# Second layer norm: cast and square of the next token chunk issued ahead of the normalization of the current one

## The chip, the cores and the metric

The kernel runs on 8 cores of one Trainium2 chip. Each core computes one of the 8 batch entries by itself, with its own copy of the weights, and no core waits for another. The metric is the device time in microseconds (us) of the slowest core.

## The reference

The reference is one transformer layer on x of shape (8, 2048, 1024): an RWKV attention block and a mixture of experts, each behind a layer norm without learned scale. Cut to what matters:

```
x = x + attention(layernorm(x))          # time mix, k/v/r projections, wkv scan, output projection
x = x + ffn(layernorm(x))                # the second layer norm is the stage that is changed

layernorm(x): m = mean(x); v = var(x); (x - m) / sqrt(v + 1e-5)      # over the 1024 channels
ffn(h): shared = (silu(conv3(h)) * (h @ shared_up)) @ shared_down
        routed = top-2 of 16 experts by softmax(h @ router_w); expert 15 is the identity
        every other expert e: (silu(h @ gate[e]) * (h @ up[e])) @ down[e], weighted by combine[:, e]
```

## The kernel before

Everything is held with channels on the 128 partitions (8 blocks of 128 channels, `cc`) and tokens along the free axis (T = 2048). The residual `acc` is an SBUF tensor of 128 x 8 x 2048 f32 that lives through the whole kernel. The program is a row of blocks, and at each block's end all engines meet at a barrier:

- the attention block (lines 150 to 400 or so): four chunks of 512 tokens with layer norm, projections and scan;
- `blk2`, the second layer norm (lines 445 to 503), which reads `acc` and writes `ln2x` in bf16;
- `blk3`, the router (logits by TensorE at L533, softmax and top-2 on VectorE), whose result goes to DRAM;
- `blk4`, the conv and shared expert (L665 to L684), then 15 experts: gate L700, up L714, down L726, each over all 2048 tokens in four PSUM banks, with Silu at L798, the products at L768 and L769 and the adds to `acc` at L777. Behind it one DMA (L805) writes the output.

In `blk2` the 2048 tokens go in four chunks, `g_` = 0 to 3, of 512. There is one of every buffer: `accb` (the chunk in bf16), `xsqb` (its square), `m_sb` (mean), `vr_sb` (variance, then reciprocal deviation), `sgl` (a scratch row) and two PSUM banks `pc[0]` and `pc[1]`. One chunk is a chain over three engines:

1. VectorE casts 128 x 4096 elements of `acc` to `accb` (L463) and squares them into `xsqb` (L464).
2. TensorE multiplies with a matrix of ones, 8 matmuls into `pc[0]` (L494, the sum over channels) and 8 into `pc[1]` (L498, the sum of squares). Its marks are `S2_` and `SQ2_` with the chunk's number.
3. VectorE makes mean and variance with four small instructions (L466 to L470).
4. ScalarE makes the reciprocal deviation with Ln and Exp (L484, L485).
5. VectorE normalizes: for each of the 8 channel blocks a subtraction (L473) and a multiplication (L474), 16 instructions.

The order of the work is the order in which each engine's code is written; there is no scheduler. The helper `ES.do` makes every VectorE instruction wait for the one before it. TensorE waits in chunk `g_` for the square (`cast2_`) and, from chunk 1 on, for the normalization of the chunk before (`norm`). Since VectorE casts a chunk only when the chunk before is normalized, the first of these waits includes the second.

GpSimd issues nine weight loads at the start of `blk2` (L447 to L456): conv, shared up and down, router weights and bias, and four expert slots. The router's TensorE code waits for the first five.

Of the kernel before, what the change touches and what calls it, by code (L numbers as in the profile page):

```python
# [58 lines left out]
def build_one(ms, rec, stop_after="ffn", taps=(), parts=("id", "sh", "ex")):  # L59
# [31 lines left out]
    with ExitStack() as st:  # L91
# [327 lines left out]
        with ExitStack() as s2:  # L419
# [15 lines left out]
            with ExitStack() as sb2:  # L435
                eb2 = sb2.enter_context
                accb = eb2(nc.sbuf_tensor("accb", [128, CC, 512], BF16))
                xsqb = eb2(nc.sbuf_tensor("xsqb", [128, CC, 512], BF16))
                m_sb = eb2(nc.sbuf_tensor("m_sb", [128, 512], F32))
                vr_sb = eb2(nc.sbuf_tensor("vr_sb", [128, 512], F32))  # L440
                sgl = eb2(nc.sbuf_tensor("sgl", [128, 512], F32))
                pc = [eb2(nc.psum_tensor(f"pc{i}", [128, 512], F32)) for i in range(2)]
                blk2 = eb2(nc.Block())

                @blk2.gpsimd
                def _(g):
                    g.dma_start(cwS[:], cw_d.rearrange("k (cc p) o -> p (k cc) o", p=128)).then_inc(s_dwf, 16)  # L447
                    g.dma_start(suS[:], su_d.rearrange("(cc p) o -> p cc o", p=128)).then_inc(s_dwf, 16)
                    g.dma_start(sdS[:], sd_d.rearrange("(cc p) o -> p cc o", p=128)).then_inc(s_dwf, 16)
                    g.dma_start(rwS[:], rw_d.rearrange("(cc p) o -> p cc o", p=128)).then_inc(s_dwf, 16)  # L450
                    g.dma_start(rbS[:], rb_d[:]).then_inc(s_dwf, 16)
                    for m in range(4):
                        e, j = m // 3, m % 3
                        src = (gw_d, uw_d, dw_d)[j]
                        view = src[e].rearrange("(cc p) o -> p cc o", p=128)
                        g.dma_start(slot_ap(m), view).then_inc(s_dsl[m % 4], 16)  # L456

                @blk2.vector
                def _(v):
                    VS.eng = v  # L460
                    for g_ in range(4):
                        gs = slice(g_ * 512, (g_ + 1) * 512)
                        VS.do(lambda gs=gs: v.tensor_copy(accb[:], acc[:, :, gs]), f"cast{g_}")  # L463
                        VS.do(lambda: v.tensor_tensor(xsqb[:], accb[:], accb[:], OP.mult), f"cast2_{g_}")  # L464
                        v.wait_ge(s_pe, MS(f"t:SQ2_{g_}"))
                        VS.do(lambda: v.tensor_scalar_mul(m_sb[:], pc[0][:], 1.0 / C))  # L466
                        VS.do(lambda: v.tensor_tensor(vr_sb[:], m_sb[:], m_sb[:], OP.mult))
                        VS.do(lambda: v.scalar_tensor_tensor(vr_sb[:], pc[1][:], 1.0 / C, vr_sb[:],
                                                             OP.mult, OP.subtract))
                        VS.do(lambda: v.tensor_scalar_add(vr_sb[:], vr_sb[:], EPS), f"var2_{g_}")  # L470
                        v.wait_ge(s_sc, MS(f"s:rstd2_{g_}"))
                        for cc in range(CC):
                            VS.do(lambda cc=cc, gs=gs: v.tensor_tensor(sgl[:], acc[:, cc, gs], m_sb[:], OP.subtract))  # L473
                            VS.do(lambda cc=cc, g_=g_: v.tensor_tensor(  # L474
                                ln2x[:, cc, 2 + g_ * 512: 2 + (g_ + 1) * 512], sgl[:], vr_sb[:], OP.mult))
                        VS.ms[f"v:norm{g_}"] = VS.v
                    VS.do(lambda: v.memset(ln2x[:, :, 0:2], 0.0), "ln2pad")

                @blk2.scalar
                def _(s):  # L480
                    SS.eng = s
                    for g_ in range(4):
                        s.wait_ge(s_dv, MS(f"v:var2_{g_}"))
                        SS.do(lambda: s.activation(vr_sb[:], vr_sb[:], AF.Ln))  # L484
                        SS.do(lambda: s.activation(vr_sb[:], vr_sb[:], AF.Exp, scale=-0.5), f"rstd2_{g_}")  # L485

                @blk2.tensor
                def _(t):
                    for g_ in range(4):
                        t.wait_ge(s_dv, MS(f"v:cast2_{g_}"))  # L490
                        if g_ >= 1:
                            t.wait_ge(s_dv, MS(f"v:norm{g_ - 1}"))
                        for cc in range(CC):
                            inst = t.matmul(pc[0][:], ones_b[:], accb[:, cc, :],  # L494
                                            start=(cc == 0), stop=(cc == CC - 1))
                        TS_.mark(inst, f"S2_{g_}")
                        for cc in range(CC):
                            inst = t.matmul(pc[1][:], ones_b[:], xsqb[:, cc, :],  # L498
                                            start=(cc == 0), stop=(cc == CC - 1))
                        TS_.mark(inst, f"SQ2_{g_}")  # L500
# [353 lines left out]
```

## Time and profile before

| | |
|---|---|
| time, median of 2 runs | 2940.83 us (2889.86 and 2991.81) |
| the profiled execution | 2889.95 us |
| its span, slowest core (core 3) | 2888.4 us |
| spans of the other cores | 2870.7 to 2885.7 us |
| TensorE, VectorE, ScalarE busy on core 3 | 1872.4, 1278.9, 326.9 us |
| second layer norm on core 3 | from 840.7 to 953.7 us |

The trace comes from one execution, and its times count from the core's first instruction. The second row is that execution's own time. An engine's busy time is the sum of its instructions. In a row of the timeline, the number in brackets is how long the engine had been idle before the instruction, and behind the arrow stands what released it.

### The profile page before, as it was taken

The numbers are of one execution on the slowest core, as the hardware profiler recorded it, in microseconds if no ns is written. First come the engines' busy times: TensorE is split into PE (matmuls) and PEld (weight loads), VectorE is DVE, ScalarE is ACT, GpSimd is POOL, SyncE is SP. The second block draws the span as 40 slices with busy tenths as digits, with TensorE's granted clock in tenths as the row PEclk, the third lists the DMA queues.
The fourth block names the chain that finished last, engine by engine and source line by source line (L and its number), as shares of the span: only waits on it lengthen the run. The fifth ranks groups of instructions, "written<-read, shape, count | busy, mean of one in ns | idle before, by whom it ended". The sixth has DMA issues, their size and how long they took to land.

```text
span 2888.4 us, 21639 instructions; the slowest of 8 cores (2870.7 to 2888.4 us)
## 1 busy us (share of the span) xinstructions
PE 1872.4 (65%) x7648; PEld 784.1 (27%) x7648; DVE 1278.9 (44%) x1772; ACT 326.9 (11%) x551; POOL 67.9 (2%) x88
## 2 busy tenths in 40 slices
PE   2415424226022579887887888878878878888885
PEld 1202101102010234333333333333333323333332
DVE  4474574584456441242442442433433434424433
ACT  0310220310410000001001001000000010010000
POOL 0000000000010000000000000000000000000000
PEclk8656767668566789998998989989989889989887
DMA  6603404305035000032131221321321321212203
GB/s 147 97 20 51 66 0 63 53 0 88 0 45 87 17 7 1 0 51 37 16 46 23 35 37 16 51 37 15 51 37 15 52 31 21 39 25 40 30 1 116
DMA packets 69194, 112.77 MB, mean 39 GB/s; under 512 B 2480, under 2 KB 37312, under 8 KB 68048
## 3 DMA queue, kind: packets, MB, share of 16 engines
q0 software_dynamic: 63856, 94.50, 22.0%
q1 hardware_dynamic: 5232, 16.91, 1.8%
q8 instruction: 61, 1.00, 0.1%
q14 instruction: 45, 0.37, 0.1%
HBM read 197.28 MB, written 8.52 MB: 71 GB/s over the span
## 4 chain that ended last, share of the span: by engine, by line
PE 52%; DVE 9%; issue 2%; ACT 1%; DVEq 0%; DMA 0%; ACTq 0%; POOLq 0%
PE pc L700 18%; PE pc L726 16%; PE pc L714 14%; DVE h L769 4%; DVE sg L768 4%; PE pc L665 2%; PE pc L684 1%; ACT sg L798 1%; PE pc L673 1%; DVE h L739 1%; DVE acc L742 1%; DVE h L751 0%; DVE acc L777 0%; DVEq L36 0%; DMA cb<-comb_dram 0%
## 5 line engine op out<-in xcount | busy, mean ns | idle before, releaser
L700 PE MATMUL pc<-ln2x,wsl 128*128 128x512 bf16 x1920 | 519.7, 437 | 190.9 <-ACT sg L798 189.9
L768 DVE TENSOR_TENSOR sg<-sg,pc 128x512 f32<-128x512 f32 x240 | 165.0, 687 | 822.2 <-PE pc L714 803.2
L726 PE MATMUL pc<-h,wsl 128*128 128x512 bf16 x1920 | 461.5, 404 | 100.6 <-DVE h L769 99.9
L714 PE MATMUL pc<-ln2x,wsl 128*128 128x512 bf16 x1920 | 427.6, 379 | 0.0
L777 DVE TENSOR_TENSOR acc<-acc,pc 128x512 f32<-128x512 f32 x480 | 330.2, 688 | 182.8 <-PE pc L726 144.3
L700 PEld LDWEIGHTS pc<-ln2x,wsl 128*128 128x128 bf16 x1920 | 206.7, 110 | 502.8 <-issue 341.4
L798 ACT ACTIVATE sg<-pc 128x512 f32<-128x512 f32 x240 | 143.3, 597 | 1522.4 <-PE pc L700 1016.2
L726 PEld LDWEIGHTS pc<-h,wsl 128*128 128x128 bf16 x1920 | 190.2, 103 | 371.9 <-issue 192.2
L369 PE MATMUL pb<-mx,wsla 128*128 128x512 bf16 x512 | 131.6, 425 | 240.8 <-DVE mx L225 214.5
L714 PEld LDWEIGHTS pc<-ln2x,wsl 128*128 128x128 bf16 x1920 | 187.6, 98 | 230.2
L769 DVE TENSOR_TENSOR h<-sg,cb 128x512 bf16<-128x512 f32 x240 | 166.1, 692 | 25.4 <-DVE sg L768 0.5
L369 PE MATMUL pb<-sry,wsla 128*128 128x512 bf16 x256 | 66.6, 429 | 143.2 <-DVE sry L282 94.9
L369 PEld LDWEIGHTS pb<-mx,wsla 128*128 128x128 bf16 x512 | 54.1, 107 | 318.2 <-issue 279.4
L369 PE MATMUL pb<-mxb,wsla 128*128 128x512 bf16 x256 | 63.9, 416 | 64.3 <-DMA wsla<-wv 57.8
L665 PE MATMUL pc<-ln2x,cw_sb 128*128 128x512 bf16 x384 | 86.2, 386 | 9.6 <-PEq L515 6.4
L360 PE MATMUL pb<-xb,ones_b 128*128 128x512 bf16 x32 | 14.0, 618 | 102.1 <-DVE xsq L200 102.1
L369 PEld LDWEIGHTS pb<-sry,wsla 128*128 128x128 bf16 x256 | 27.2, 107 | 182.7 <-issue 164.1
L275 DVE TENSOR_TENSOR_SCAN Q_ch<-ewb,Q_ch,e_t 128x128 f32<-128x128 f32 x128 | 62.0, 484 | 13.7 <-DVE Q_ch L275 0.5
L271 DVE TENSOR_TENSOR_SCAN P_ch<-ewb,P_ch,w 128x128 f32<-128x128 f32 x128 | 62.0, 484 | 13.7 <-DVE P_ch L271 0.5
L260 DVE CAST v_sb<-pb 128x512 bf16<-128x512 f32 x32 | 22.1, 692 | 99.3 <-PE pb L369 96.4
L494 PE MATMUL pc<-accb,ones_b 128*128 128x512 bf16 x32 | 13.9, 616 | 80.3 <-DVE xsqb L464 80.3
L281 DVE TENSOR_TENSOR w<-w,e_t 128x1024 f32<-128x1024 f32 x16 | 19.6, 1226 | 97.2 <-ACT e_t L328 97.2
(119 smaller groups left out, 922.8 us busy)
## 6 DMA issues: line engine op xcount, KB each, us to landing
wsl<-gw POOLq DMA_DIRECT2D x15, 1024.0 KB, 10.1
wsl<-uw POOLq DMA_DIRECT2D x15, 1024.0 KB, 10.4
wsl<-dw POOLq DMA_DIRECT2D x15, 1024.0 KB, 10.1
acc<-x SPq DMA_DIRECT2D x4, 2048.0 KB, 24.6
wsla<-wk POOLq DMA_DIRECT2D x4, 2048.0 KB, 17.1
wsla<-wv POOLq DMA_DIRECT2D x4, 2048.0 KB, 18.4
wsla<-wr POOLq DMA_DIRECT2D x4, 2048.0 KB, 28.2
wsla<-wo POOLq DMA_DIRECT2D x4, 2048.0 KB, 16.7
```

The source lines that it names most:

```text
L271: VS.do(lambda cc=cc: v.tensor_tensor_scan(P_ch[:, cc, 1:], ewb[:, cc, :], w1[:, cc, :], P_ch[:, cc, 0:1], OP.mult, OP.add))
L275: VS.do(lambda cc=cc: v.tensor_tensor_scan(Q_ch[:, cc, 1:], ewb[:, cc, :], e_t[:, cc, :], Q_ch[:, cc, 0:1], OP.mult, OP.add))
L369: inst = t.matmul(pb[od][:], wsl_a[m % 2][:, kc, od * 128:(od + 1) * 128], rhs_t[:, kc, :], start=(kc == 0), stop=(kc == CC - 1))
L665: inst = t.matmul(pc4[ocI][:], cwS[:, kk * 8 + kc, ocI * 128:(ocI + 1) * 128], ln2x[:, kc, t0 - 2 + kk: t0 - 2 + kk + 512], start=(kk == 0 ...
L673: inst = t.matmul(pc4[4 + ocI][:], suS[:, kc, ocI * 128:(ocI + 1) * 128], ln2x[:, kc, t0:t0 + 512], start=(kc == 0), stop=(kc == CC - 1))
L700: inst = t.matmul(pc4[tc][:], slot_ap(3 * e)[:, kc, ocI * 128:(ocI + 1) * 128], ln2x[:, kc, 2 + tc * 512: 2 + (tc + 1) * 512], start=(kc = ...
L714: inst = t.matmul(pc4[4 + tc][:], slot_ap(3 * e + 1)[:, kc, ocI * 128:(ocI + 1) * 128], ln2x[:, kc, 2 + tc * 512: 2 + (tc + 1) * 512], sta ...
L726: inst = t.matmul(pc4[(oc % 2) * 4 + tc][:], slot_ap(3 * e + 2)[:, kcI, oc * 128:(oc + 1) * 128], h[:, kcI, tc * 512:(tc + 1) * 512], star ...
L768: VS.do(lambda sl=sl, tc=tc: v.tensor_tensor(sl[:], sl[:], pc4[4 + tc][:], OP.mult))
L769: VS.do(lambda sl=sl, e=e, ocI=ocI, tc=tc: v.tensor_tensor(h[:, ocI, tc * 512:(tc + 1) * 512], sl[:], cb[e % 2][:, tc, :], OP.mult), f"h{e ...
L777: VS.do(lambda dst=dst, ac=ac, oc=oc, tc=tc: v.tensor_tensor(dst, ac, pc4[(oc % 2) * 4 + tc][:], OP.add))
L798: SS.do(lambda idx=idx, tc=tc: s.activation(sg[idx % 2][:], pc4[tc][:], AF.Silu), f"silu{e}_{ocI}_{tc}")
```

## The change

The edit is in VectorE's and TensorE's code of `blk2`. The cast and the square of chunk 0 stand ahead of the loop. Inside the loop, the cast and the square of chunk `g_ + 1` stand between the variance of chunk `g_` and the wait for its reciprocal deviation. TensorE's wait for the normalization of the chunk before is taken out. No instruction is added, and none is dropped.

```diff
                     VS.eng = v
+                    VS.do(lambda: v.tensor_copy(accb[:], acc[:, :, 0:512]), "cast0")
+                    VS.do(lambda: v.tensor_tensor(xsqb[:], accb[:], accb[:], OP.mult), "cast2_0")
                     for g_ in range(4):
                         gs = slice(g_ * 512, (g_ + 1) * 512)
-                        VS.do(lambda gs=gs: v.tensor_copy(accb[:], acc[:, :, gs]), f"cast{g_}")
-                        VS.do(lambda: v.tensor_tensor(xsqb[:], accb[:], accb[:], OP.mult), f"cast2_{g_}")
                         v.wait_ge(s_pe, MS(f"t:SQ2_{g_}"))
...
                         VS.do(lambda: v.tensor_scalar_add(vr_sb[:], vr_sb[:], EPS), f"var2_{g_}")
+                        if g_ + 1 < 4:
+                            ns = slice((g_ + 1) * 512, (g_ + 2) * 512)
+                            VS.do(lambda ns=ns: v.tensor_copy(accb[:], acc[:, :, ns]), f"cast{g_ + 1}")
+                            VS.do(lambda: v.tensor_tensor(xsqb[:], accb[:], accb[:], OP.mult), f"cast2_{g_ + 1}")
                         v.wait_ge(s_sc, MS(f"s:rstd2_{g_}"))
...
                         t.wait_ge(s_dv, MS(f"v:cast2_{g_}"))
-                        if g_ >= 1:
-                            t.wait_ge(s_dv, MS(f"v:norm{g_ - 1}"))
```

VectorE, the first chunk of `blk2`, before. The names are those of the buffers above, and in brackets stand the semaphores of an instruction's waits (`s_pe` from TensorE, `s_sc` from ScalarE, `s_dv` VectorE's own):

```order
L463 CAST accb<-acc 128x4096 [waits s_dv]
L464 TENSOR_TENSOR xsqb<-accb 128x4096 [waits s_dv]
L466 TENSOR_SCALAR m_sb<-pc 128x512 [waits s_pe,s_dv]
L467 TENSOR_TENSOR vr_sb<-m_sb 128x512 [waits s_dv]
L468 SCALAR_TENSOR_TENSOR vr_sb<-pc,vr_sb 128x512 [waits s_dv]
L470 TENSOR_SCALAR vr_sb<-vr_sb 128x512 [waits s_dv]
L473 TENSOR_TENSOR sgl<-acc,m_sb 128x512 [waits s_sc,s_dv]
L474 TENSOR_TENSOR ln2x<-sgl,vr_sb 128x512 [waits s_dv]
```

The same place in the changed kernel:

```order
L461 CAST accb<-acc 128x4096 [waits s_dv]
L462 TENSOR_TENSOR xsqb<-accb 128x4096 [waits s_dv]
L466 TENSOR_SCALAR m_sb<-pc 128x512 [waits s_pe,s_dv]
L467 TENSOR_TENSOR vr_sb<-m_sb 128x512 [waits s_dv]
L468 SCALAR_TENSOR_TENSOR vr_sb<-pc,vr_sb 128x512 [waits s_dv]
L470 TENSOR_SCALAR vr_sb<-vr_sb 128x512 [waits s_dv]
L473 CAST accb<-acc 128x4096 [waits s_dv]
L474 TENSOR_TENSOR xsqb<-accb 128x4096 [waits s_dv]
L477 TENSOR_TENSOR sgl<-acc,m_sb 128x512 [waits s_sc,s_dv]
L478 TENSOR_TENSOR ln2x<-sgl,vr_sb 128x512 [waits s_dv]
```

The cast and the square of chunk 1 (now L473 and L474) have moved in between the variance and the first instruction that waits for ScalarE (now L477).

VectorE where chunk 0 ends and chunk 1 goes on, before (the last pair of the normalization, then what follows):

```order
L473 TENSOR_TENSOR sgl<-acc,m_sb 128x512 [waits s_dv]
L474 TENSOR_TENSOR ln2x<-sgl,vr_sb 128x512 [waits s_dv]
L463 CAST accb<-acc 128x4096 [waits s_dv]
L464 TENSOR_TENSOR xsqb<-accb 128x4096 [waits s_dv]
L466 TENSOR_SCALAR m_sb<-pc 128x512 [waits s_pe,s_dv]
L467 TENSOR_TENSOR vr_sb<-m_sb 128x512 [waits s_dv]
```

The same place in the changed kernel:

```order
L477 TENSOR_TENSOR sgl<-acc,m_sb 128x512 [waits s_dv]
L478 TENSOR_TENSOR ln2x<-sgl,vr_sb 128x512 [waits s_dv]
L466 TENSOR_SCALAR m_sb<-pc 128x512 [waits s_pe,s_dv]
L467 TENSOR_TENSOR vr_sb<-m_sb 128x512 [waits s_dv]
L468 SCALAR_TENSOR_TENSOR vr_sb<-pc,vr_sb 128x512 [waits s_dv]
L470 TENSOR_SCALAR vr_sb<-vr_sb 128x512 [waits s_dv]
```

The wait for TensorE (L466) used to follow the square directly; now the 16 instructions of the normalization stand between them. TensorE's own order is the same in both kernels.

## Rows read from the trace of the kernel before

**Rows 1.** Page: span and busy times by engine.
```profile
span 2888.4 us, 21639 instructions; the slowest of 8 cores (2870.7 to 2888.4 us)
PE 1872.4 (65%) x7648; PEld 784.1 (27%) x7648; DVE 1278.9 (44%) x1772; ACT 326.9 (11%) x551; POOL 67.9 (2%) x88
```
**Rows 2.** Waits, 840.5 to 954 us: engine, line, releaser, us in total, times, longest.
```profile
DVE m_sb L466 <- PE pc L498: 23.5, 4, 6.6
DVE sgl L473 <- ACT vr_sb L485: 8.3, 4, 2.9
```
**Rows 3.** Timeline, chunk 1: start, us, engine, line, op, [idle before, releaser].
```profile
856.69 0.69 DVE L473 TENSOR_TENSOR sgl<-acc,m_sb 128x512 f32<-128x512 f32 x1 [2.95 <-ACT vr_sb L485]
...
869.43 2.29 DVE L463 CAST accb<-acc 128x4096 bf16<-128x4096 f32 x1
871.83 2.29 DVE L464 TENSOR_TENSOR xsqb<-accb 128x4096 bf16<-128x4096 bf16 x1
...
874.38 3.57 PE L494 MATMUL pc<-accb,ones_b 128*128 128x512 bf16 x8 [23.64 <-DVE xsqb L464]
...
877.74 2.75 PE L498 MATMUL pc<-xsqb,ones_b 128*128 128x512 bf16 x8
...
880.67 0.69 DVE L466 TENSOR_SCALAR m_sb<-pc 128x512 f32<-128x512 f32 x1 [6.55 <-PE pc L498]
...
885.16 0.69 DVE L473 TENSOR_TENSOR sgl<-acc,m_sb 128x512 f32<-128x512 f32 x1 [1.67 <-ACT vr_sb L485]
```
**Rows 4.** Timeline: the same two waits in chunks 0, 2 and 3, and the stage's end.
```profile
850.91 0.69 DVE L466 TENSOR_SCALAR m_sb<-pc 128x512 f32<-128x512 f32 x1 [5.50 <-PE pc L498]
...
908.56 0.69 DVE L466 TENSOR_SCALAR m_sb<-pc 128x512 f32<-128x512 f32 x1 [5.97 <-PE pc L498]
...
913.40 0.69 DVE L473 TENSOR_TENSOR sgl<-acc,m_sb 128x512 f32<-128x512 f32 x1 [2.02 <-ACT vr_sb L485]
...
936.34 0.69 DVE L466 TENSOR_SCALAR m_sb<-pc 128x512 f32<-128x512 f32 x1 [5.52 <-PE pc L498]
...
953.60 0.07 DVE L477 MEMSET ln2x<- 128x16 bf16 x1
...
954.14 8.95 PE L533 MATMUL pc<-ln2x,rw_sb 128*16 128x512 bf16 x32 [17.98 <-PEq L435]
```
**Rows 5.** Timeline: the first cast and GpSimd's weight loads.
```profile
840.73 2.29 DVE L463 CAST accb<-acc 128x4096 bf16<-128x4096 f32 x1 [0.39 <-PEq L125]
841.06 3.00 POOL L447 DMA_DIRECT2D cw_sb<-cw  x1 [138.59 <-SPq L435]
...
846.53 0.56 POOL L451 DMA_DIRECT2D rb_sb<-rb  x1
...
849.58 0.95 POOL L456 DMA_DIRECT2D wsl<-gw  x1
```
**Rows 6.** DMA view of 780 to 1300 us: the router bias, KB, us from issue to landing.
```profile
rb_sb<-rb POOLq DMA_DIRECT2D x1, 0.1 KB, 50.1
```
**Rows 7.** One line's instructions (L742, TensorE busy beside it): ns min/median/max.
```profile
L742 DVE TENSOR_TENSOR acc<-acc,h x4: 4424/4425/4425, 1003.8 to 1031.0; 128x4096 f32<-128x4096 f32 x4
```
**Rows 8.** Window ahead of the router: us, busy PE, PEld, DVE, ACT, POOL (x), PEclk, DMA share, GB/s.
```profile
945.00:953.90 8.90, 0.00 (x0) 0.00 (x0) 7.49 (x12) 0.00 (x0) 0.00 (x0) 0.50 0.00 0
```
**Rows 9.** Chain that ended last, start and us: a gate group at its usual shortest, and the longest.
```profile
1283.49 7.06 PE pc L700 x32
...
2201.31 10.02 PE pc L700 x32
```
**Rows 10.** Page, costliest groups: the gate matmuls.
```profile
L700 PE MATMUL pc<-ln2x,wsl 128*128 128x512 bf16 x1920 | 519.7, 437 | 190.9 <-ACT sg L798 189.9
```
**Rows 11.** The gate matmuls on cores 3 and 7: count, ns, first and last start.
```profile
L700 PE MATMUL pc<-ln2x,wsl x1920: 376/379/634, 1172.2 to 2815.7; 128*128 128x512 bf16 x192
L700 PE MATMUL pc<-ln2x,wsl x1920: 376/379/634, 1155.9 to 2799.4; 128*128 128x512 bf16 x192
```

## The prediction

> **What bounds the kernel now.** I read the page first. Of a span of 2888.4 us on core 3, TensorE is busy 1872.4 and VectorE 1278.9 us [rows 1], so neither is busy throughout and the kernel is a chain of stages that hand work to each other. The stage that the change touches is the second layer norm. Its first cast starts at 840.73 us [rows 5] and its last instruction, a memset, at 953.60 [rows 4]: 112.9 us, 3.9% of the span. It ends in a barrier, and TensorE begins the router 0.5 us behind it, at 954.14, after 17.98 us of idleness [rows 4]. So what the stage gives up, the router starts earlier by.
>
> Next I read the waits of this stage. VectorE waits 23.5 us in four goes for the sums from TensorE and 8.3 us in four goes for the reciprocal deviation from ScalarE [rows 2]. These 31.8 us are all that VectorE waits there, apart from the gaps of about 0.1 us between its instructions; the other 81 us are its own work. VectorE therefore bounds the stage, with two round trips per chunk added in series. The timeline of chunk 1 shows the series [rows 3]: cast and square from 869.43, TensorE's 16 matmuls from 874.38 to 880.49, VectorE idle for 6.55 us until 880.67, four small instructions, idle for 1.67 us until 885.16, then the normalization. The reader should note that TensorE sat idle for 23.64 us before its matmuls. It has room for the sums, but gets its input too late.
>
> **The change, part by part.** All instructions and their sizes stay; only VectorE's order changes. I go through the two waits.
>
> *The wait for TensorE.* In chunk 0 nothing can be put ahead of it, so its 5.50 us [rows 4] stay. In chunks 1, 2 and 3 the square is done before the normalization of the chunk before begins. That normalization takes from 856.69 to 869.43, 12.74 us for 16 instructions of 0.69 us and their gaps (on to the start of the cast behind it) [rows 3]. TensorE's work takes 6.1 us (874.38 to 877.74 + 2.75 [rows 3]). It ends about 6 us before VectorE asks for it, so even a doubling of it would be hidden. Removed are 6.55 [rows 3] + 5.97 + 5.52 [rows 4] = 18.04 us.
>
> *The wait for ScalarE.* The cast and square of the next chunk, 4.8 us from 869.43 to 871.83 + 2.29 + gap [rows 3], now run while ScalarE works. ScalarE's part took 2.95 us in chunk 0 (with the load of its table), 1.67 in chunk 1 [rows 3] and 2.02 in chunk 2 [rows 4]. All three are shorter than 4.8 us, so 6.64 us go. Chunk 3 has no next chunk, and its wait stays.
>
> *What comes in their place.* Each of the six waits becomes an ordinary gap, 0.1 us by the pair of cast and square (871.83 - 869.43 - 2.29) [rows 3]: 0.6 us back. *The wait taken out of TensorE* costs and brings nothing by itself: what it named had to be done anyway before the new square. The moved cast writes `accb` only after TensorE has read it, and VectorE has just waited for that at L466, so no wait is added.
>
> The sum: 18.04 + 6.64 - 0.6 = 24.1 us. The memset then starts near 929.5 instead of 953.60.
>
> *The unknown costs.* First, VectorE's normalization now runs beside TensorE's matmuls, which the stage has not shown before. The nearest row is a relative of the subtraction, an addition of two SBUF operands at 128x4096 with TensorE busy beside it: 4.42 us [rows 7]. A cost of 0.69 us for 512 columns [rows 3] and 4.42 for 4096 [rows 7] differ by 1.04 ns a column, and that rate leaves 0.16 us of the 0.69 as a fixed part: a small and plausible one, so the instruction beside TensorE is not visibly slowed. I take nothing. The other end is bounded by the overlap: 3 x 6.1 = 18 us of VectorE work, and if all of it went a quarter slower, 4.6 us. Below nothing is excluded, since no operand shrinks. Second, the router starts earlier, and it needs the router bias, issued at 846.53 and landing 50.1 us behind its issue, so near 897 [rows 5, 6]. That is 33 us before 929.5, so I take nothing. Third, TensorE is idle before the router for some 24 us instead of 18: the sums of chunk 3 now end ahead of the 3 us of small instructions, the ScalarE wait and the last normalization. Its granted clock was already 0.50 in the 8.9 us before the router [rows 8], which is the lower of its two levels, 1.2 GHz. It can fall no further, so again nothing. Fourth, everything behind the router keeps its order and its gaps and shifts by 24 us.
>
> Against the profiled execution, 2889.95 - 24.1 = 2865.9 us. That execution agrees with the lower of the two runs shown (2889.86 us); their median, 2940.83, is drawn up by the other (2991.81). The ratio, 0.9917, is what I expect to hold; the absolute time holds for executions like the profiled one. A median of two that again had one run 102 us longer would be 2865.9 + 51 = 2917. A difference of 2%, 58 us, is about what a measurement of this kernel can tell from no change, so this gain lies within it.
>
> **The rivals.** *The clock takes it back (slower).* The expert stage works with pauses in which TensorE's clock falls. A gate group of 32 matmuls takes 7.06 us right behind the down projection and up to 10.02 behind a wait [rows 9]. All of L700 costs 519.7 us [rows 10]; without 15 groups of 7.06 there are 413.8 us for 45 groups, 9.20 each. If starting the stage at another moment put all 45 at 10.02, this would add 45 x 0.82 = 37 us, and the kernel would end at 2889.95 - 24.1 + 37 = 2903. The point from which it decides is 24.1 / 45 = 0.54 us per group. Against it speaks that cores 3 and 7 begin the gates at 1172.2 and 1155.9 us, 16.3 us apart, and their last gate matmul starts 1643.5 us behind the first on both [rows 11]: the groups do not care when the stage begins. The Trainium skill speaks for this rival. Its page "TensorE: Matmul & The Clock Gate", in the part on the HAM clock gate, says that the activity window is free-running and does not reset when the kernel starts; by that rule the moment of the start would matter, up to the price just worked out. The two cores' rows disagree with it at this size, so I give the rival little.
>
> *Weights late (half the gain, or none).* If the bias landed behind 929.5, the router would wait. Half of the gain is gone if it lands at 941.5, 95 us after its issue instead of 50: the time would be 2878. What speaks for it is the first load's issue, which took 3.00 us from 841.06 while the cast that began at 840.73 ran for 2.29 us; the last took 0.95 [rows 5]. The moved casts come at 853.8 and later, behind the last issue (849.58 + 0.95), but inside the time in which the loads move. If each of the three moved casts held the loads up by its length, that would be 6.9 us, landing at 903.5: still 26 us early. In the Trainium skill, "SBUF — State Buffer", section "SBUF: two separate sides", a cast in a 2-port mode locks GpSimd out while it runs and starves the descriptors of its DMAs; the 3.00 us agree, and by that rule the landing moves by no more than these 6.9 us.
>
> *The gain drowns in the other stages.* Core 3 alone sets the time, and the cores' spans lie between 2870.7 and 2888.4 us [rows 1], 17.7 us apart with the same program. If the slowest core in another execution comes 12 to 24 us later, 2878 to 2890 is measured; if all come like the fastest, 2848.
>
> *The change does not do what it says.* VectorE could still stand still at L466 if TensorE began late. It does not: its only wait is for the square, and its queue holds nothing else. I leave 2 in 100 for no gain, 2890.
>
> **How the numbers follow.** The forecast, 24 us off, gets 0.74. The gain drowned or doubled by the spread gets 0.12, half to either side; weights late 0.05; the clock rival 0.05; no effect 0.02; something unseen 0.02. The likeliest's own range is 2857 to 2875 (the 4.6 us of slower VectorE work and as much spread above, all 31.8 us of waits gone below). The range of 8 in 10 reaches down to 2850 for an execution with all cores early and up to 2920, which takes in the rivals at 2878, 2890 and 2903 and the median of two unlike runs, 2917. Faster by over 2% would need 58 us where only 31.8 us of waits exist, so only a measurement against an unlike run gives it: 0.04. Slower by over 2% needs 82 us of loss after the gain, more than the clock rival has: 0.03. Within 2%: 0.93.
>
> **What would show it right or wrong.** In the profile of the changed kernel the stage from the first cast to the memset should take 88.8 us instead of 112.9. VectorE's waits for TensorE should be one of 5.5 us, and those for ScalarE one of 1.7 us. TensorE's matmuls for chunks 1 to 3 should run beside L477 and L478, which should still take 0.69 us. The router should start 0.5 us behind the memset, with no wait for a DMA. From there to the end, the distance should be unchanged at 2888.4 - 954.1 = 1934.3 us. I am wrong if a wait for the sums above 1 us is left in chunks 1 to 3, if the normalization's instructions grow, or if that distance moves by more than 5 us.

## The result, and the profile after

The changed kernel takes 0.9924 of the time of the kernel before, with a 95% interval of 0.9911 to 0.9937. That is 22 us less (18 to 26), within the 2% that count as the same. The runs of before lie between 2889.45 and 2892.79 us, those of after between 2864.84 and 2870.55 us. Some executions of any kernel are several per cent longer, with a lower clock on the cores of one die; they are left out of every time and ratio here, and of their profiles only the cores of the other die are read.

The profiled execution took 2865.14 us, with a span of 2863.6 us on core 5. First the page: busy times are those of before to within 3.1 us, as they should be when nothing is added or dropped [rows 1].

```profile
span 2863.6 us, 21636 instructions; the slowest of 8 cores (2848.7 to 2863.6 us)
PE 1875.5 (65%) x7648; PEld 784.5 (27%) x7648; DVE 1278.9 (45%) x1772; ACT 327.0 (11%) x551; POOL 67.9 (2%) x88
```

The waits of VectorE in the stage (engine, line, what it waited for, us in total, times, longest) answer to [rows 2]. L466 is the same line as before, L477 is the former L473:

```profile
DVE m_sb L466 <- PE pc L500: 5.5, 1, 5.5
DVE sgl L477 <- ACT vr_sb L489: 1.7, 1, 1.7
```

Of four waits each, one each is left: 7.2 us where there were 31.8. The timeline from chunk 0's variance to chunk 2 answers to [rows 3] and [rows 4]:

```profile
852.12 0.69 DVE L466 TENSOR_SCALAR m_sb<-pc 128x512 f32<-128x512 f32 x1 [5.54 <-PE pc L500]
...
855.05 2.29 DVE L473 CAST accb<-acc 128x4096 bf16<-128x4096 f32 x1
855.08 1.28 ACT L488 ACT_TABLE_LOAD   x1 [38.69 <-DVE vr_sb L470]
856.38 0.63 ACT L488 ACTIVATE vr_sb<-vr_sb 128x512 f32<-128x512 f32 x1
857.10 0.63 ACT L489 ACTIVATE vr_sb<-vr_sb 128x512 f32<-128x512 f32 x1
857.45 2.29 DVE L474 TENSOR_TENSOR xsqb<-accb 128x4096 bf16<-128x4096 bf16 x1
859.85 0.69 DVE L477 TENSOR_TENSOR sgl<-acc,m_sb 128x512 f32<-128x512 f32 x1
859.89 3.57 PE L496 MATMUL pc<-accb,ones_b 128*128 128x512 bf16 x8 [7.94 <-DVE xsqb L474]
860.64 0.69 DVE L478 TENSOR_TENSOR ln2x<-sgl,vr_sb 128x512 bf16<-128x512 f32 x1
...
863.25 2.10 PE L500 MATMUL pc<-xsqb,ones_b 128*128 128x512 bf16 x8
...
872.58 0.69 DVE L466 TENSOR_SCALAR m_sb<-pc 128x512 f32<-128x512 f32 x1
...
896.32 2.29 DVE L473 CAST accb<-acc 128x4096 bf16<-128x4096 f32 x1 [0.46 <-DVE vr_sb L470]
...
918.34 0.69 DVE L477 TENSOR_TENSOR sgl<-acc,m_sb 128x512 f32<-128x512 f32 x1 [1.67 <-ACT vr_sb L489]
...
931.11 0.07 DVE L481 MEMSET ln2x<- 128x16 bf16 x1
...
931.65 8.87 PE L535 MATMUL pc<-ln2x,rw_sb 128*16 128x512 bf16 x32 [25.19 <-PEq L435]
```

ScalarE's table load and its two instructions end at 857.73, under the cast and the square, which end at 859.74. TensorE's sums run from 859.89 to 865.35, beside the normalization, and L466 at 872.58 finds them ready: the row has no bracket. The normalization's instructions still take 0.69 us with TensorE beside them. One stall is new: VectorE sits idle for 0.46 us ahead of the cast at 896.32, where the gaps between its other instructions are 0.1 us.

The stage, from the first cast at 841.89 to the memset, takes 89.2 us where it took 112.9. The profiled executions differ by 24.8 us, and it can be added up: the stage -23.65 us; the slowest core enters it 1.16 us later (841.89 and 840.73); from the memset to the issue of the output 1910.1 and 1910.3, -0.2; the output's landing 22.1 us behind its issue on core 5 and 24.2 on core 3, -2.1. The issue on core 5 is this row:

```profile
L807 SPq DMA_DIRECT2D out<-acc x1: 389/389/389, 2841.2 to 2841.2; - x1
```

### The profile page after: what moved, and what is told of

It is laid out like the page before. It is cut to its first block, busy times and chain, and to the rows that moved or that the text cites. A ratio compares the mean times of both kernels' runs of the same rounds, so it can differ in the third digit from the quotient of the medians.

```text
span 2863.6 us, 21636 instructions; the slowest of 8 cores (2848.7 to 2863.6 us)
## 1 busy us (share of the span) xinstructions
PE 1875.5 (65%) x7648; PEld 784.5 (27%) x7648; DVE 1278.9 (45%) x1772; ACT 327.0 (11%) x551; POOL 67.9 (2%) x88
## 4 chain that ended last, share of the span: by engine, by line
PE 53%; DVE 10%; issue 2%; ACT 1%; DVEq 0%; DMA 0%; ACTq 0%; POOLq 0%
PE pc L702 18%; PE pc L728 16%; PE pc L716 15%; DVE h L771 4%; DVE sg L770 4%; PE pc L667 2%; PE pc L686 1%; ACT sg L800 1%; PE pc L675 1%; DVE acc L744 1%; DVE h L741 1%; DVE acc L779 0%; DVE h L753 0%; DVEq L36 0%; DMA cb<-comb_dram 0%
## 5 line engine op out<-in xcount | busy, mean ns | idle before, releaser
L260 DVE CAST v_sb<-pb 128x512 bf16<-128x512 f32 x32 | 22.1, 692 | 99.0 <-PE pb L369 96.1
L281 DVE TENSOR_TENSOR w<-w,e_t 128x1024 f32<-128x1024 f32 x16 | 19.6, 1226 | 97.6 <-ACT e_t L328 97.6
L369 PEld LDWEIGHTS pb<-mxb,wsla 128*128 128x128 bf16 x256 | 27.0, 107 | 101.0 <-issue 77.1
```

What stands on the lines that cost most here:

```text
L369: inst = t.matmul(pb[od][:], wsl_a[m % 2][:, kc, od * 128:(od + 1) * 128], rhs_t[:, kc, :], start=(kc == 0), stop=(kc == CC - 1))
```

## The experiments

Each experiment's diff is against the changed kernel, where nothing else is said. "Stage" is the time from the first cast to the memset, and "rest" the time from the memset to the issue of the output's DMA; both are read from every core's instruction rows and named for the majority of the cores.

### TensorE's wait alone

Against the kernel before, only this:

```diff
                         t.wait_ge(s_dv, MS(f"v:cast2_{g_}"))
-                        if g_ >= 1:
-                            t.wait_ge(s_dv, MS(f"v:norm{g_ - 1}"))
```

> The kernel before, with only TensorE's wait for the normalization of the chunk before taken out; VectorE's order is that of before. Theory (the gain comes from VectorE's order, the wait was implied by the square): the stage of the second layer norm stays at 112.9 us, VectorE still waits 4 times for TensorE, 23.5 us in all, and the time stays at 2890 us. Rival (the wait itself held TensorE back): the waits for TensorE shrink by some us and the stage gets shorter than 110 us.

On cores 4 to 7 the stage takes 112.7 or 112.8 us and the rest is 1910.4 us, for 112.9 and 1910.3 us on most cores before. The waits on core 5:

```profile
DVE m_sb L466 <- PE pc L496: 23.4, 4, 6.5
DVE sgl L473 <- ACT vr_sb L485: 8.3, 4, 3.0
```

Taking the wait out does nothing while VectorE keeps its order. There is no total time of this kernel that could be compared, so this is shown for the stage and the rest alone.

### The cast behind the wait for ScalarE

```diff
+                        v.wait_ge(s_sc, MS(f"s:rstd2_{g_}"))
                         if g_ + 1 < 4:
                             ns = slice((g_ + 1) * 512, (g_ + 2) * 512)
                             VS.do(lambda ns=ns: v.tensor_copy(accb[:], acc[:, :, ns]), f"cast{g_ + 1}")
                             VS.do(lambda: v.tensor_tensor(xsqb[:], accb[:], accb[:], OP.mult), f"cast2_{g_ + 1}")
-                        v.wait_ge(s_sc, MS(f"s:rstd2_{g_}"))
```

> The changed kernel, with the cast and the square of the next chunk behind the wait for the reciprocal deviation instead of ahead of it, still ahead of the normalization. Theory (two separate round trips, 18.0 and 6.6 us): the wait for TensorE stays hidden in chunks 1 to 3, the wait for ScalarE returns in chunks 0 to 2 (2.95 + 1.67 + 1.67, less 0.3 of gaps), so the stage takes 89.2 + 6.0 = 95.2 us and the whole gain over before is 17.7 us, ratio 0.994. Rival (VectorE does not keep its pace when TensorE works beside it, and the two terms only happen to add up): the stage comes out away from 95.2 by more than 1 us.

The stage takes 95.1 or 95.2 us on seven cores, 6.0 more than with the full change. The waits on core 5:

```profile
DVE accb L474 <- ACT vr_sb L489: 6.6, 3, 2.9
DVE m_sb L466 <- PE pc L500: 5.5, 1, 5.5
DVE sgl L477 <- ACT vr_sb L489: 1.7, 1, 1.7
```

So the two terms are separate: this order keeps the whole TensorE term and gives back the ScalarE term, 6.6 us less two gaps of 0.1 us and the 0.46 us stall. Two runs took 2870.97 and 2873.04 us against 2887.4 to 2888.9 of before, which is 14 to 18 us less; they are too few for an interval. The rest was 1914.3 us on five cores and 1907.6 to 1908.1 on three, where it had been 1910.1: a clear sign that the stages behind do care.

### TensorE's wait put back

```diff
                         t.wait_ge(s_dv, MS(f"v:cast2_{g_}"))
+                        if g_ >= 1:
+                            t.wait_ge(s_dv, MS(f"v:norm{g_ - 1}"))
```

> The changed kernel, with TensorE's wait for the normalization of the chunk before put back; VectorE keeps the new order. Theory: TensorE's sums of chunks 1 to 3 can't run beside the normalization, VectorE waits about 6 us for each of them, and only the ScalarE term is left: the stage takes 89.2 + 17.5 = 106.7 us, the time is 5 to 7 us below before, ratio 0.998. The rival that TensorE's wait costs nothing once the square is early: the stage stays at 89.2 us and the ratio at 0.992.

The stage takes 108.2 to 108.4 us. Timeline of VectorE and TensorE on core 3:

```profile
870.79 3.57 PE L498 MATMUL pc<-accb,ones_b 128*128 128x512 bf16 x8 [20.69 <-DVE ln2x L478]
874.16 2.53 PE L502 MATMUL pc<-xsqb,ones_b 128*128 128x512 bf16 x8
876.87 0.69 DVE L466 TENSOR_SCALAR m_sb<-pc 128x512 f32<-128x512 f32 x1 [6.22 <-PE pc L502]
...
903.81 0.69 DVE L466 TENSOR_SCALAR m_sb<-pc 128x512 f32<-128x512 f32 x1 [6.58 <-PE pc L502]
...
931.11 0.69 DVE L466 TENSOR_SCALAR m_sb<-pc 128x512 f32<-128x512 f32 x1 [6.59 <-PE pc L502]
```

TensorE now starts when the normalization ends, and VectorE waits 24.9 us in four goes. With the new order on VectorE, this wait, which cost nothing before, costs 19 us: both halves of the edit are needed. It is 1.6 us more than expected, mostly since the three waits came to 19.4 us and not to the 18.04 us of before: fewer of the sums ran at the upper clock level (6.22, 6.58 and 6.59 us for 6.55, 5.97 and 5.52 [rows 3, 4]).

The total was a miss. The ratio to before is 1.0002 (0.9987 to 1.0016), and 0.998 was expected. The stage is 4.6 us shorter than before, but the rest is 1914.9 us on five cores against 1910.3 before and gives it back (on two cores it is 1908.1 us and on one 1918.3). This is the clock rival of the prediction, at a size that I had put aside; the rows that tie it to the clock stand in the last experiment.

### The sums made twice

```diff
-                        for cc in range(CC):
-                            inst = t.matmul(pc[0][:], ones_b[:], accb[:, cc, :],
-                                            start=(cc == 0), stop=(cc == CC - 1))
-                        TS_.mark(inst, f"S2_{g_}")
-                        for cc in range(CC):
-                            inst = t.matmul(pc[1][:], ones_b[:], xsqb[:, cc, :],
-                                            start=(cc == 0), stop=(cc == CC - 1))
+                        for rp in range(2):
+                            for cc in range(CC):
+                                inst = t.matmul(pc[0][:], ones_b[:], accb[:, cc, :],
+                                                start=(cc == 0), stop=(cc == CC - 1))
+                            for cc in range(CC):
+                                inst = t.matmul(pc[1][:], ones_b[:], xsqb[:, cc, :],
+                                                start=(cc == 0), stop=(cc == CC - 1))
                         TS_.mark(inst, f"SQ2_{g_}")
```

> The changed kernel, with all 16 matmuls of sums made twice in each chunk (the second pass writes the same sums), so TensorE's work in the stage doubles. Theory (12.7 us of normalization cover the sums): in chunk 0 VectorE waits 3.5 to 6.8 us longer (16 more matmuls at 0.218 or 0.427 us), in chunks 1 to 3 TensorE needs 9.6 to 12.9 us and VectorE waits for nothing or under 1 us. The stage takes 92.7 to 97 us. Rival (the cover is already used up, the sums are only just hidden): each of chunks 1 to 3 gets 3 us or more of wait, and the stage takes over 101 us.

The stage takes 92.6 to 93.2 us. Timeline of chunks 0 and 1, on core 3:

```profile
853.99 0.69 DVE L466 TENSOR_SCALAR m_sb<-pc 128x512 f32<-128x512 f32 x1 [8.97 <-PE pc L500]
...
861.75 3.57 PE L497 MATMUL pc<-accb,ones_b 128*128 128x512 bf16 x8 [7.94 <-DVE xsqb L474]
...
868.75 1.89 PE L500 MATMUL pc<-xsqb,ones_b 128*128 128x512 bf16 x8
874.45 0.69 DVE L466 TENSOR_SCALAR m_sb<-pc 128x512 f32<-128x512 f32 x1
```

Only chunk 0 pays, 3.5 us: VectorE has no other wait for the sums in the stage. In chunk 1 the doubled sums end at 870.64, still 3.8 us ahead of VectorE. TensorE's time in chunks 1 to 3 is free now, and apart from the first wait for TensorE and the last for ScalarE the stage is bound by VectorE alone. The one run took 2866.97 us.

### The weight loads in the other order

```diff
-                    g.dma_start(cwS[:], cw_d.rearrange("k (cc p) o -> p (k cc) o", p=128)).then_inc(s_dwf, 16)
                     g.dma_start(suS[:], su_d.rearrange("(cc p) o -> p cc o", p=128)).then_inc(s_dwf, 16)
+                    g.dma_start(cwS[:], cw_d.rearrange("k (cc p) o -> p (k cc) o", p=128)).then_inc(s_dwf, 16)
```

> The changed kernel, with GpSimd's first two weight loads in the other order: shared up (1 MB) first, conv (3 MB) second. If the first load's issue took 3.00 us because the cast held GpSimd up, the shared up load, now first and under the cast, takes until the cast's end or longer, over 2.2 us instead of 0.88, and the conv load about as long as its size asks. If the 3.00 us come from the load's own size, the shared up load stays near 0.9 us and the conv load near 3.0 us in second place. Either way the stage stays at 89.2 us and the time at 2865 to 2870 us.

Timeline of the cast and of GpSimd beside it, core 0:

```profile
840.82 2.29 DVE L461 CAST accb<-acc 128x4096 bf16<-128x4096 f32 x1 [0.39 <-PEq L125]
...
841.16 2.44 POOL L447 DMA_DIRECT2D su_sb<-su  x1 [138.75 <-SPq L435]
843.58 1.42 POOL L448 DMA_DIRECT2D cw_sb<-cw  x1
```

The same two loads in the changed kernel, core 5:

```profile
842.23 3.00 POOL L447 DMA_DIRECT2D cw_sb<-cw  x1 [138.83 <-SPq L435]
845.22 0.88 POOL L448 DMA_DIRECT2D su_sb<-su  x1
```

Both expectations named a part of it. The shared up load takes 2.44 us under the cast and 0.88 behind it; the conv load takes 3.00 under the cast and 1.42 behind it. The first place adds 1.56 us to the one and 1.58 to the other, whatever the load, and that is 0.4 us less than the 1.95 us for which issue and cast overlap (841.16 to 843.11). The swap by itself leaves one rival: the first load also follows 138.8 us in which GpSimd was idle, and could be slow for that. An earlier load of the changed kernel speaks against it:

```profile
263.50 0.87 POOL L160 DMA_DIRECT2D wsla<-wv  x1 [145.41 <-PE pb L369]
```

Behind 145.41 us of idleness, and with no cast of this length beside it, it takes 0.87 us. The load at 845.22 runs beside the square of chunk 0 and still takes 0.88 us, so it is the cast that holds the issue and not VectorE's work as such. The rule of the Trainium skill, "SBUF — State Buffer", section "SBUF: two separate sides", that such a cast locks GpSimd out, agrees with these rows. In the changed kernel no moved cast meets an issue: the last load is issued at 850.74 for 0.95 us, and the first moved cast starts at 855.05. The router bias landed 44.7 us behind its issue on core 5, for 50.1 [rows 6]. The stage is 89.1 or 89.2 us on six cores and 0.6 more on two, where without the swap one core had the 0.6 us. The one run took 2864.92 us, as expected.

### A wider normalization

```diff
-                sgl = eb2(nc.sbuf_tensor("sgl", [128, 512], F32))
+                sgl = eb2(nc.sbuf_tensor("sgl", [128, CC, 256], F32))
...
-                        for cc in range(CC):
-                            VS.do(lambda cc=cc, gs=gs: v.tensor_tensor(sgl[:], acc[:, cc, gs], m_sb[:], OP.subtract))
-                            VS.do(lambda cc=cc, g_=g_: v.tensor_tensor(
-                                ln2x[:, cc, 2 + g_ * 512: 2 + (g_ + 1) * 512], sgl[:], vr_sb[:], OP.mult))
+                        for hf in range(2):
+                            h0 = g_ * 512 + hf * 256
+                            mbc = m_sb[:, hf * 256:(hf + 1) * 256].unsqueeze(1).broadcast_to([128, CC, 256])
+                            rbc = vr_sb[:, hf * 256:(hf + 1) * 256].unsqueeze(1).broadcast_to([128, CC, 256])
+                            VS.do(lambda h0=h0, mbc=mbc: v.tensor_tensor(
+                                sgl[:], acc[:, :, h0:h0 + 256], mbc, OP.subtract))
+                            VS.do(lambda h0=h0, rbc=rbc: v.tensor_tensor(
+                                ln2x[:, :, 2 + h0:2 + h0 + 256], sgl[:], rbc, OP.mult))
```

> The changed kernel, with the normalization of a chunk in 4 instructions of 128 x 2048 (8 blocks of 256 tokens, mean and deviation broadcast over the blocks) instead of 16 of 128 x 512; the scratch tensor grows to 128 x 8 x 256 f32. Theory (VectorE alone bounds the stage now, so its fixed costs count one to one): 4 instructions at 2048 x 1.04 ns + 0.16 us = 2.29 us and 0.1 of gap each are 9.6 us for 12.74, four times: 12.6 us less. The stage takes 76.6 us, the sums (6.1 us) stay hidden, the time falls to 2853 us by the profiled execution, ratio to before 0.987. Rival (the freed time turns into waits for TensorE, since less work covers the sums): waits at L466 in chunks 1 to 3 appear, and the stage stays above 80 us.

The subtractions of the stage on core 6 (count, then busy us and mean ns of one, then idle time before them); the multiplications take the same 18.3 and 2292:

```profile
L480 DVE TENSOR_TENSOR sgl<-acc,m_sb 128x2048 f32<-128x2048 f32 x8 | 18.3, 2292 | 2.4 <-ACT vr_sb L493 1.7
```

One instruction takes 2292 ns, the expected 2.29 us. The stage takes 76.2 us on most cores (13.0 less), and the waits are again one of 5.5 and one of 1.7 us. On the engine that bounds a stage, a fixed cost of 0.16 us and a gap of 0.1 us per instruction count one to one: 48 instructions fewer make 12.5 us, and the 0.46 us stall is gone too. The ratio to before is 0.9871 (0.9856 to 0.9886), as expected, but more closely than its parts: the rest was 1912.8 us on four cores, 2.7 us longer, and 1906.0 to 1909.9 us on the others.

### And the square on ScalarE

Beside the wide normalization:

```diff
-                            VS.do(lambda: v.tensor_tensor(xsqb[:], accb[:], accb[:], OP.mult), f"cast2_{g_ + 1}")
...
+                        if g_ + 1 < 4:
+                            s.wait_ge(s_dv, MS(f"v:cast{g_ + 1}"))
+                            SS.do(lambda: s.activation(fl(xsqb[:]), fl(accb[:]), AF.Square), f"sq{g_ + 1}")
...
-                        t.wait_ge(s_dv, MS(f"v:cast2_{g_}"))
+                        t.wait_ge(s_dv, MS(f"v:cast{g_}"))
...
+                        t.wait_ge(s_sc, MS(f"s:sq{g_}"))
```

Chunk 0 is changed in the same way.

> As the wide normalization, and with the square of the chunk on ScalarE (Square from bf16 to bf16) instead of VectorE; TensorE's first 8 matmuls wait only for the cast. Theory: VectorE loses 2.4 us of work in each of chunks 1 to 3; in chunk 0 the square (about 3.5 us) runs beside the first 8 matmuls and 1 to 2 us go; the wait for ScalarE in chunk 0 comes back by 0.5 us since the cast alone covers 2.4 of its 2.95 us. The stage takes about 68.5 us, the time is 2845 us, ratio 0.984. Rival (ScalarE becomes the bound: square behind the deviation, and the activation table is reloaded at 1.28 us a switch): VectorE waits for the sums in chunks 1 to 3 and the stage stays above 74 us.

The ratio to before is 0.9834 (0.9821 to 0.9848), the fastest version of this study; its five runs took 2839.14 to 2844.01 us. Chunk 0 on core 0:

```profile
843.90 1.28 ACT L489 ACT_TABLE_LOAD   x1 [27.95 <-DVE accb L461]
843.91 3.57 PE L503 MATMUL pc<-accb,ones_b 128*128 128x512 bf16 x8 [9.24 <-DVE accb L461]
...
845.19 3.62 ACT L489 ACTIVATE xsqb<-accb 128x4096 bf16<-128x4096 bf16 x1
...
848.95 3.57 PE L508 MATMUL pc<-xsqb,ones_b 128*128 128x512 bf16 x8 [1.47 <-ACT xsqb L489]
...
852.70 0.69 DVE L465 TENSOR_SCALAR m_sb<-pc 128x512 f32<-128x512 f32 x1 [8.93 <-PE pc L508]
```

The stage takes 70.1 us on seven cores and 68.4 on one, where 68.5 was expected. What I had left out is in these rows: the table load of 1.28 us now stands ahead of the square of chunk 0, and TensorE's second eight matmuls behind its pause of 1.47 us run at the lower clock throughout (3.57 us for 1.89). On core 5, the one with 68.4 us, they follow a pause of 1.53 us and take 1.89. There is only one load in the stage, and Square, Ln and Exp alternate behind it without another. That the total came out at the expected place is luck: the rest was 1904.7 to 1905.4 us on six cores, 5 us shorter than before, and 1908.8 on the two others, the slowest core among them.

### Does the rest care when it begins?

Two kernels with idle work at the end of the stage, 2 instructions as shown, and 4:

```diff
                     VS.do(lambda: v.memset(ln2x[:, :, 0:2], 0.0), "ln2pad")
+                    for _ in range(2):
+                        VS.do(lambda: v.tensor_tensor(sgl[:], m_sb[:], m_sb[:], OP.mult))
```

> The changed kernel, with 2 more VectorE instructions of 128x512 at the end of the stage (they write a scratch row that nobody reads), which start the router 1.6 us later. Theory of the prediction (the stages behind do not care when they begin): the distance from the memset to the output's issue grows by 1.6 us, from 1910.1 to 1911.7 on most cores, and router and experts keep 39.4 and 1643.5 us. Rival (TensorE's clock level depends on the moment at which its work begins): the router part changes by 1 to 4 us, as it did in the runs with the cast behind the deviation and with TensorE's wait put back (42.3 and 42.8 us for 39.4), or the gates' stretch moves by 3 us or more on most cores.

> The same with 4 more instructions, a shift of 3.2 us. Theory of the prediction: 1913.3 us from the memset to the output's issue, router 39.4 us behind its start and gates' stretch 1643.5 us. Rival: as above; whether this shift falls on a better or a worse moment than the one of 1.6 us I can't say beforehand, only that the two runs and the changed kernel will not all agree.

With the shift of 3.2 us, six cores have a rest of 1913.6 or 1913.7 us, near the expected 1913.3 (two have 1917.6). With 1.6 us the cores fall apart: 1903.7, 1907.2, 1910.0, 1913.4 twice, 1914.0, 1916.8 and 1916.9 us, where 1911.7 was expected. The runs took 2866.85 us with 1.6 us and 2871.01 us with 3.2, one of each. The router of core 3, first in the changed kernel, then with 1.6 us, then with 3.2 us:

```profile
918.12 8.86 PE L535 MATMUL pc<-ln2x,rw_sb 128*16 128x512 bf16 x32 [25.20 <-PEq L435]
930.58 5.66 PE L541 MATMUL pc<-id_sb,lg 16*128 16x16 f32 x32 [3.60 <-DVE lg L557]
946.00 5.14 PE L547 MATMUL pc<-id_sb,ctm 128*16 128x128 f32 x32 [9.77 <-DVE ctm L579]
```
```profile
926.28 9.73 PE L537 MATMUL pc<-ln2x,rw_sb 128*16 128x512 bf16 x32 [26.82 <-PEq L435]
939.62 6.97 PE L543 MATMUL pc<-id_sb,lg 16*128 16x16 f32 x32 [3.60 <-DVE lg L559]
956.70 6.43 PE L549 MATMUL pc<-id_sb,ctm 128*16 128x128 f32 x32 [10.11 <-DVE ctm L581]
```
```profile
918.08 8.96 PE L537 MATMUL pc<-ln2x,rw_sb 128*16 128x512 bf16 x32 [28.40 <-PEq L435]
930.64 5.57 PE L543 MATMUL pc<-id_sb,lg 16*128 16x16 f32 x32 [3.60 <-DVE lg L559]
946.33 5.06 PE L549 MATMUL pc<-id_sb,ctm 128*16 128x128 f32 x32 [10.12 <-DVE ctm L581]
```

The same three pieces of TensorE work take 19.7, 23.1 and 19.6 us. They follow pauses of nearly the same length (25 to 28, 3.60 and about 10 us); what differs is the moment at which they start. Over the time from the router's first matmul to the first of the convolution (window and its length in us, then busy time of TensorE, its weight loads, VectorE, ScalarE and GpSimd, then the mean granted clock, the DMA share and GB/s), in the changed kernel and with 1.6 us:

```profile
918.10:957.50 39.40, 19.66 (x96) 12.58 (x97) 11.64 (x24) 1.70 (x2) 0.00 (x0) 0.72 0.03 4
926.30:969.50 43.20, 23.12 (x96) 14.51 (x97) 11.64 (x24) 1.70 (x2) 0.00 (x0) 0.62 0.03 4
```

VectorE and ScalarE are busy for the same time in both. The mean granted clock is 0.72 and 0.62 of full speed, and 0.72 again with 3.2 us: the upper level holds for 17.1, 10.2 and 17.1 us of the three windows. The experts move too: the gates' stretch from first to last matmul is 1643.5 us in the changed kernel and between 1633.7 and 1644.3 us on the cores with the 1.6 us shift. The shortest and the longest gates' stretch of these kernels, core 7 with the shift of 1.6 us and core 7 with TensorE's wait put back:

```profile
1139.90:2773.70 1633.80, 1348.95 (x5600) 565.81 (x5601) 633.34 (x920) 140.94 (x236) 41.33 (x54) 0.90 0.20 31
1166.70:2813.20 1646.50, 1362.57 (x5599) 569.13 (x5600) 633.34 (x920) 140.90 (x236) 41.33 (x54) 0.89 0.21 31
```

Again only TensorE's busy time differs, by 13.6 us for 12.7 us of stretch.

With the shifts the cores don't fall apart at random. Ahead of the inserted instructions, VectorE's first wait in the stage is 5.5 or 5.6 us on some cores, where the clock first rises 8.0 to 8.3 us behind the first cast, and 6.05 to 6.08 us on the others, where it rises 9.1 or 9.2 us behind it. With 1.6 us the five cores of the first kind have a router of 43.2 to 43.7 us and the three others one of 40.7 to 42.0; with 3.2 us the six of the first kind have 39.7 to 40.1 us and the two others 42.5 and 42.9. The five begin the stage between 821.0 and 835.9 us, so the router's time goes with the shift and the kind of core and not with the time since the core's start. The gates' stretch doesn't follow from them: 1637.4 to 1644.3 us on those five.

The commonest values over the kernels of this study, and where a few cores stand apart, theirs:

| kernel | stage, us | router, us | gates' stretch, us | rest, us |
|---|---|---|---|---|
| before | 112.9 | 39.5 | 1643.5, on one 1646.5 | 1910.3, on one 1913.7 |
| changed | 89.2 | 39.4 | 1643.5, on one 1640.1 | 1910.1, on one 1907.2 |
| TensorE's wait alone (four cores) | 112.8 | 39.5 | 1643.5 | 1910.4 |
| cast behind the wait for ScalarE | 95.2 | 42.4 | 1644.2 or 1643.5, on three 1637.2 | 1914.3, on three 1907.6 to 1908.1 |
| TensorE's wait put back | 108.3 | 42.8 | 1644.2, on two 1637.3 | 1914.9, on two 1908.1, on one 1918.3 |
| sums made twice | 92.7 | 39.4 | 1643.5 | 1910.0 to 1910.6, on one 1906.6, on one 1913.4 |
| weight loads swapped | 89.2 | 39.4 | 1643.5 | 1910.1, on three 1907.2, 1910.7 and 1913.5 |
| wide normalization | 76.2 | 40.7 | 1644.3 | 1912.8, on four 1906.0 to 1909.9 |
| square on ScalarE | 70.1 | 43.4 | 1634.1 | 1905.3, on two 1908.8 |
| shift of 1.6 us | 89.2 | 40.7 to 43.7 | 1633.7 to 1644.3 | 1903.7 to 1916.9 |
| shift of 3.2 us | 89.2 | 39.7 | 1643.8 | 1913.6, on two 1917.6 |

"Router" is the time from its first matmul to the first of the convolution. An edit of a few us in front of this part can thus come out up to 8 us better or worse than the edit itself is worth (1903.7 for 1911.7 on one core here; 1918.3 for 1910.3 on one core with TensorE's wait put back). That the levels of the clock make the difference is read from the rows above. For the router, which shift brings which level is shown for two shifts and the two kinds of core; why, and what decides it in the experts, stays open.

## Why the prediction was right or wrong

**The sum.** The stage was to take 88.8 us and takes 89.2. The term for TensorE (18.04 us) and that for ScalarE (6.64 us) both hold: the waits left are 5.5 and 1.7 us, as forecast for chunk 0 and chunk 3. The term for the gaps was 0.6 us, and one of the six came out at 0.46 us instead of 0.1; before, this stall sat in the ScalarE wait of chunk 2 (2.02 us for 1.67 [rows 3, 4]), and I had booked its 0.35 us as removed. The experiments with one half each confirm that the terms add up: 6.0 us come back without the ScalarE half, and TensorE's wait put back costs 19 us.

**The time.** 2865.9 us were forecast, the profiled execution took 2865.14 and the other runs 2864.84 to 2870.55. The forecast ratio of 0.9917 lies inside the interval of 0.9911 to 0.9937. That the profiled execution matches to 0.8 us is part luck: the slowest core entered the stage 1.2 us later and its output landed 2.1 us sooner. From the router's first matmul to the end it took 1932.0 us on that core, for the 1934.3 us of the prediction, and the landing makes 2.1 us of that difference. Four of the other six runs took 2869.29 to 2870.55 us; none of them was profiled, so where their 4 to 5 us lie is not shown.

**The unknown costs.** VectorE's normalization beside TensorE was put at nothing, with 4.6 us as the other end: 0.69 us an instruction in both, so nothing is right. The weights were put at nothing, and the router started 0.54 us behind the memset. The idle time before the router was put at 24 us and is 25.2.

**The step that was wrong.** It is the fourth unknown cost, "everything behind the router keeps its order and its gaps and shifts by 24 us", and with it the dismissal of the clock rival: "the groups do not care when the stage begins". I drew it from cores 3 and 7, which begin the gates 16.3 us apart and have the same stretch [rows 11]. Core 4 of the same trace contradicts it: its gates take 1646.5 us and its rest 1913.7. The conclusion held for this change (1910.1 us for 1910.3 on most cores), but not as a rule: a shift of 1.6 us spread the rest over 13 us, and two other orders of the same instructions moved it by +4 or -2.5 us and by +4.6 us on most cores. That it held here was luck in part: of the other versions in the table, three stay at 1910 to 1911 us on most cores and the others don't. What two cores of one program share is more than the instructions: they also share the whole pattern of work and pauses ahead of the gates, and an edit changes that. This is my reading of why cores 3 and 7 misled me; no run separates it from others. The range for the likeliest case, 2857 to 2875, should have carried up to 8 us more on either side for the clock, which is what single cores moved by. The rival's size of 37 us was too large all the same: the largest loss seen on any core was 8.0 us.

**The rule on the clock.** The prediction set cores 3 and 7 against a rule of the Trainium skill, "TensorE: Matmul & The Clock Gate", in its part on the HAM clock gate: the window runs free and doesn't reset with the kernel. These runs don't settle it. By that rule the moment of a piece of work matters, and with the shift of 1.6 us it does. But cores whose clock ran free of their work would see it rise at scattered moments of it. In the changed kernel the first casts lie between 826.1 and 841.9 us, and the clock first rises 8.0 or 8.1 us behind the cast on seven cores and 9.2 us on core 6. How the cores come to share this is not shown.

## What to carry to other kernels

When the engine that bounds a stage waits in series for two others, put the input of the next round ahead of the wait for the current one: with one buffer each it works as long as the reader of that buffer is already known to be done, and the engine waits only at the start and at the end. Such a reordering needs both sides, VectorE's new order and the removal of TensorE's now binding wait; either alone shortened the stage by 0 to 5 us of the 24. Once only one engine bounds the stage, count its fixed cost per instruction: merging the 16 normalization instructions of each chunk into 4 brought another 13 us, and the sums stayed hidden.

Before a gain or loss under some 8 us on this kernel is explained, read stage by stage whether TensorE's work behind the edit kept its time, since its clock alone can give or take that much.

## What the hardware showed that I had not expected

- The stages behind the edit take 1903.7 to 1918.3 us for the same instructions, depending on what comes before, with VectorE and ScalarE busy for the same time; the three pieces of the router take 19.6 or 23.1 us behind pauses of nearly the same length.
- Before, in the changed kernel and with the shifts, cores that begin the stage up to 16 us apart see TensorE's clock first rise 8.0 to 8.3 us behind their first cast, or 9.1 or 9.2 us. In the kernels with a shift the router's time goes with which of the two it is.
- GpSimd's issue of a DMA is held by a cast on VectorE for 1.6 us, for a 1 MB load (2.44 for 0.88 us) as for a 3 MB load (3.00 for 1.42 us); 145 us of idleness ahead of an issue don't lengthen it (0.87 us).
- One VectorE instruction in the stage starts 0.35 us late, before and after: the 51st of its instructions there. It is the normalization's first subtraction of chunk 2 before (idle 2.02 for 1.67 us) and the last cast after (0.46 for 0.1 us). The lateness stays at the place in the program and not with the work, in the run with doubled sums too, and the stages with the wide normalization, which have 41 and 37 instructions, have no such gap. What it is was not tried.
